# Routing spread over four steps with three sends in each, and the first norm's rows on ScalarE

## The chip, the cores and the metric

The kernel runs on one core of a Trainium2 chip. The metric is the device time of one execution in microseconds.

## The reference

64 sequences of 113 tokens with 128 features each. 36 tokens of a sequence come from a 96x96 image by a patch projection with shifted copies and a layer norm, 77 are text. Then an attention block and a block of experts, both on a layer norm and both with a residual:

```python
h = _L0_tok_ref(x, ...)                      # patches 16x16, shifted projections, layer norm
h = jnp.concatenate([h, txt], axis=1)        # (64, 36 + 77, 128)
h = h + _L0_attn_ref(_layernorm(h), ...)     # 8 heads of 64; scores and softmax in bfloat16
h = h + _L0_ffn_ref(_layernorm(h), ...)      # a shared expert and 3 of 16 experts per token

# in _L0_ffn_ref
affinity = sigmoid(xf @ gate_w.T)
_, sel = top_k(affinity + expert_bias, 3)
gating = sel_aff / (sel_aff.sum(-1) + 1e-9)
out = shared_out + einsum('tk,tkd->td', gating, sel_out)
```

## The kernel before

Each engine has its own program, written out by hand; semaphores tie them together. An engine works strictly in its program's order, so a wait holds up all that stands behind it on that engine.

**Stages.** First the image patches of eight octets (an octet is 8 sequences) are projected, normed and put into `h`. Then comes a loop of steps n = -8 to 66 (n = 8 o + k; `o` is the octet, `k` the place in it). A step works on many sequences at once, each at another stage. On step n, VectorE makes the normed row `xn` of sequence n + 8 (line 1304: row minus `mean1`, times `rs1`, both per token), TensorE transposes it (line 786), ScalarE copies the transpose to `xt` (997) and VectorE makes its rest (1331). TensorE makes q (one chunk of four sequences, into bank 1), k (bank 2) and later v (792) from `xt`, ScalarE copies q (989) and k (993). Sequence n gets its row maximum (VectorE, 1309), ScalarE doubles it to pairs (984), VectorE subtracts it (1314), ScalarE takes the exponential (1012). Sequence n - 1 gets its product with v; sequence n - 2 gets its output projection (TensorE 778), is added into `h` (VectorE 1324), gets the statistics of the second norm (1326, 1337), whose variance and power GpSimd makes (573, 575), and VectorE writes the normed row into `pay` (1360), the last of its program in a step that depends on GpSimd. Sequence n - 3 is transposed (812) and multiplied with the gate weights (836). A further matmul makes the scores of sequence n + 1 (830), which ScalarE copies (1018).

**Routing.** For each group q of four sequences VectorE chooses the three experts of each token: `route`, parts 0 to 11. Part 2 is four MAX8 (1174), part 3 four FIND_INDEX8 (1178), part 4 a cast (1181), part 5 a comparison of 113x192 (1185), part 6 the count of the chosen (1191) and a product, parts 7 to 11 small sums up to the gates. TensorE counts the ranks of the tokens within each expert (`ranks`, six small matmuls) and VectorE turns them into row numbers (`place`, parts 0 to 3, five instructions). A step has six points (0 to 5) between VectorE's other work where `routing` puts such parts in. Parts 0 to 5 stand in step n = 4q + 7, parts 6 to 11 in 4q + 8, the placement in 4q + 9 (for group 14 in 4q + 8). GpSimd then sends each sequence with three indirect DMAs, one for each choice (`send_rows`, line 606), 12 a group. `SENDS` gives the sends of each step of an octet: 0, 3, 3, 3, 3, 4, 4, 4; steps 64 and 65 have 3 and 9. The point of a send within GpSimd's step is 0, 1 or 2; points 0 and 1 come right behind line 575. Group 15 is routed and sent among the expert tiles.

**First norm.** GpSimd makes `rs1` for an octet with one power of 113x8 (`first_pow`, line 517) in step k = 6, for the octet after the next.

**Tables and tiles.** During steps 54 to 62 `full_table` derives the rows of the first 47 expert tiles from the first 12 groups. SyncE loads tiles of 256 rows (line 419) as soon as the table is there, ScalarE starts loading expert weights in step 64. In 93 tiles TensorE computes each tile (874, 885, 894), VectorE scales it and GpSimd scatters the rows (line 625). At the end everything is merged and written out.

Of the kernel before, what the change touches and what calls it, by code (L numbers as in the profile page):

```python
# [22 lines left out]
B = 64  # L23
# [8 lines left out]
OCT = 8  # L32
# [32 lines left out]
FULL_READ = {EARLY_B + 7: (("table", 2),), EARLY_B + 10: (("table", 5),), EARLY_B + 12: (("tab_done", 2),)}  # L65
FULL_AT = {EARLY_B + 6 + i: part for i, part in enumerate(((0,), (1, 2), (3, 4), (), (5, 6), (7, 8), (9, 10), (), (11,)))}
# [3 lines left out]
SENDS = (0, 3, 3, 3, 3, 4, 4, 4)  # L70
SENDS_LAST = (3, 9)
# [6 lines left out]
def build(nc, x, txt, w_feat, tok_bias, tok_gb, wq, wkv, wo, bo, gate_w, e_bias, w_ffn, out):  # L78
    ctx = ExitStack()
    with ctx:  # L80
# [74 lines left out]
        mean1 = sb("mean1", [128, B])  # L155
# [91 lines left out]
        for name in (  # L247
# [3 lines left out]
            "st1_raw st1_done mean1_done ve1_done rs1_done xn_ready xt_done xt_copied qa_done qb_done q_copied k_copied "  # L251
# [50 lines left out]
        def ok(n, end=B):  # L302

            return not isinstance(n, int) or 0 <= n < end

        def placing(o, k):

            lag = 8 if o == NOCT else 9
            return o * 2 + (k - lag) // GRP if (k - lag) % GRP == 0 and ok(o * OCT + k - lag) else None
# [132 lines left out]
        def _(pool):  # L442
# [71 lines left out]
            def first_pow(o):  # L514
# [3 lines left out]
                                        ALU.pow).then_inc(S["rs1_done"], 1)  # L518

# [70 lines left out]
            def send(o, k, point):  # L590

                if o < 1 or (o == NOCT and k >= len(SENDS_LAST)):
                    return
                sends, first = (SENDS_LAST, 0) if o == NOCT else (SENDS, 1)
                begin = sum(sends[:k])
                cuts = [0, 0, 0, sends[k]] if k % GRP == first or o == NOCT else [0, min(1, sends[k]), min(2, sends[k]), sends[k]]
                for at in range(begin + cuts[point], begin + cuts[point + 1]):
                    b, c = divmod(at, TOPK)
                    send_rows((o - 1) * OCT + b, c)
# [40 lines left out]
        def _(pe):  # L640
# [93 lines left out]
            def step(o, k):  # L734
# [28 lines left out]
                if n in FULL_AT and n <= EARLY_B + 12:  # L763
# [149 lines left out]
        def _(act):  # L913
# [49 lines left out]
            def step(o, k):  # L963
# [17 lines left out]
                if ok(n):  # L981
# [3 lines left out]
                                         ACT.Copy).then_inc(S["mx2_done"], 1)  # L985
                if ok(n + 4):
# [87 lines left out]
        def _(dve):  # L1074
# [7 lines left out]
            def first_stats(o, i):  # L1082
# [12 lines left out]
                nc.vector.tensor_copy(mean1[0:T, bass.ds(o * OCT, OCT)], mv1[0:T, :, 0]).then_inc(S["mean1_done"], 1)  # L1095
# [136 lines left out]
            def routing(o, k, point):  # L1232

                n, kk = o * OCT + k, k % GRP
                if kk == 3 and ok(n - 7) and n < B:
                    route(o * 2 + (k - 7) // GRP, ((k - 7) // GRP) % 2, point)
# [278 lines left out]
```

## Time and profile before

| | us |
|---|---|
| median of 3 runs | 939.87 |
| lowest, highest | 935.1, 944.38 |
| the profiled execution | 940.34 |
| its span | 938.6 |
| granted TensorE clock, mean | 0.86 |
| busy: TensorE | 693.4 (74%) |
| busy: VectorE | 592.6 (63%) |
| busy: ScalarE | 438.0 (47%) |
| busy: GpSimd | 547.7 (58%) |

The step of a sequence can be read from VectorE's row maximum, line 1309: it occurs once a step for n = 0 to 63. The first is at 76.02 us. A busy share over the whole span mixes the steps with the tiles; the share in one window says more. In a row the bracket at the end is the idle time of the engine just before, and who ended it. The end of a matmul is modelled, so the moment at which another engine goes on is the surer sign that it is done.

### The profile page before, as it was taken

To read this page: it belongs to the slowest core of one execution; us is meant where nothing else is said; L and a number is where in the kernel's file an instruction comes from. 1 tells how busy PE (TensorE), PEld (TensorE's weight loads), DVE (VectorE), ACT (ScalarE), POOL (GpSimd) and SP (SyncE) were. 2 spreads that over 40 slices of the span, in tenths; PEclk is the share of its full clock that TensorE was granted. 3 is DMA by queue.
4 is the path that set the end of the run, shared out by engine and by line. 5 is a ranking of instruction groups with operands and counts; after the bars stand their busy time and mean duration, and the time that the engine had idled before them with its cause. 6 is when DMAs were issued, how large, how long until landed. Compare 5 with 4: busy or idle time off the path is not lost.

```text
span 938.6 us, 19989 instructions
## 1 busy us (share of the span) xinstructions
PE 693.4 (74%) x6122; PEld 570.1 (61%) x6122; DVE 592.6 (63%) x2030; ACT 438.0 (47%) x1044; POOL 547.7 (58%) x696
## 2 busy tenths in 40 slices
PE   6657999898988989989897771787687786776100
PEld 5446887787777777777786560565555564666100
DVE  1697898898898878888888360443434443443254
ACT  2556787687776767767685320221222221221000
POOL 4452227866667676756756656555556555555464
PEclk9879999999999999989999585787778788797755
DMA  9710001100000010000104242445444444565297
GB/s 299 209 26 11 2 2 34 32 26 28 27 32 28 26 34 27 29 23 32 34 26 108 78 121 76 122 147 167 133 132 141 140 139 136 155 189 149 74 326 232
DMA packets 66444, 88.02 MB, mean 94 GB/s; under 512 B 11612, under 2 KB 58848, under 8 KB 66186
## 3 DMA queue, kind: packets, MB, share of 16 engines
q1 hardware_dynamic: 30420, 34.76, 13.5%
q10 hardware_dynamic: 23824, 28.68, 10.7%
q0 software_dynamic: 12096, 23.30, 7.4%
q8 instruction: 51, 0.84, 0.4%
q14 instruction: 53, 0.43, 0.2%
HBM read 57.32 MB, written 30.87 MB: 94 GB/s over the span
## 4 chain that ended last, share of the span: by engine, by line
PE 41%; DVE 17%; issue 12%; another core or an unknown queue 6%; POOL 5%; DMA 4%; ACT 2%; ACTq 1%; SPq 0%; DVEq 0%; POOLq 0%
PE bank L885 10%; PE bank L683 4%; PE bank L894 4%; PE bank L778 4%; DMA x2t<-expert_rows 3%; PE bank L830 3%; PE bank L723 3%; PE bank L750 2%; PE bank L874 2%; DVE mx L1309 2%; PE bank L724 2%; POOL dispatched L606 2%; DVE s L1314 1%; PE bank L792 1%
## 5 line engine op out<-in xcount | busy, mean ns | idle before, releaser
L625 POOL DMA_INDIRECT expert_rows<-yb,dst_i x186 | 182.2, 980 | 142.9 <-DVE yb L1446 91.4
L606 POOL DMA_INDIRECT dispatched<-pay,sloti x192 | 205.8, 1072 | 55.9 <-issue 54.1
L1436 DVE TENSOR_TENSOR hide<-bank,sge 128x256 f32<-128x256 f32 x93 | 39.4, 423 | 190.5 <-ACT sge L1051 138.2
L1046 ACT ACTIVATE xe<-bank 128x256 f32<-128x256 f32 x93 | 35.7, 384 | 213.3 <-remote 103.3
L885 PE MATMUL bank<-xe,kt 128*128 128x256 f32 (+1 forms) x296 | 80.0, 407 | 44.9 <-issue 44.7
L683 PE MATMUL bank<-xt,wqkv 128*128 128x452 f32 x384 | 103.7, 402 | 1.6 <-DVE xt L1331 1.2
L885 PEld LDWEIGHTS bank<-xe,kt 128*128 128x128 f32 x296 | 55.0, 226 | 52.9 <-issue 48.6
L683 PEld LDWEIGHTS bank<-xt,wqkv 128*128 128x128 f32 x384 | 70.6, 201 | 7.3 <-DVE xt L1331 1.4
L1309 DVE TENSOR_REDUCE mx<-s 113x8 bf16<-113x904 bf16 x64 | 69.6, 1088 | 6.4 <-ACT s L1018 5.6
L830 PE MATMUL bank<-kt,qt 64*113 64x113 f32 x1024 | 68.9, 272 | 4.6 <-DVE h L1324 3.6
L573 POOL TENSOR_SCALAR ve<-mv 113x1 f32<-113x1 f32 x64 | 14.8, 231 | 98.2 <-DVE mv L1337 96.9
L778 PEld LDWEIGHTS bank<-wo_r,ot 128*113 128x113 f32 x512 | 63.5, 187 | 6.8 <-ACT ot L973 2.9
L792 PE MATMUL bank<-wqkv,xt 128*113 128x512 f32 x192 | 60.7, 425 | 8.8 <-ACT qt L989 7.9
L830 PEld LDWEIGHTS bank<-kt,qt 64*113 64x113 f32 x1024 | 58.1, 176 | 12.9 <-issue 7.5
L1018 ACT ACTIVATE s<-bank 113x452 bf16<-113x452 f32 x128 | 63.2, 549 | 4.0 <-PE bank L830 3.9
L778 PE MATMUL bank<-wo_r,ot 128*113 128x128 f32 x512 | 62.4, 267 | 3.3 <-ACT ot L973 2.6
L978 ACT ACTIVATE pt<-bank 113x912 bf16<-113x912 bf16 x64 | 60.9, 952 | 3.9 <-PE bank L750 3.7
L1012 ACT ACTIVATE p<-s 113x904 bf16<-113x904 bf16 x64 | 60.7, 948 | 0.0
L1051 ACT ACTIVATE sge<-bank 128x256 f32<-128x256 f32 x93 | 35.6, 382 | 52.4 <-PE bank L885 33.8
L894 PE MATMUL bank<-kt,hide 128*128 128x128 f32 x252 | 45.8, 311 | 17.2 <-DVE hide L1436 14.5
L804 PEld LDWEIGHTS bank<-vf,pt 113*128 113x128 bf16 x512 | 47.2, 98 | 18.1 <-issue 18.1
L894 PEld LDWEIGHTS bank<-kt,hide 128*128 128x128 f32 x252 | 42.9, 221 | 25.1 <-DVE hide L1436 18.9
(209 smaller groups left out, 1829.3 us busy)
## 6 DMA issues: line engine op xcount, KB each, us to landing
kt<-in_w_ffn ACTq DMA_DIRECT2D x74, 192.0 KB
xs_all<-dispatched SPq DMA_DIRECT2D x77, 140.0 KB
x2t<-expert_rows SPq DMA_DIRECT2D x16, 672.0 KB
vr<-in_w_ffn ACTq DMA_DIRECT2D x35, 192.0 KB
out_h<-h ACTq DMA_DIRECT2D x16, 224.0 KB
x2t<-in_x ACTq DMA_DIRECT2D x4, 864.0 KB, 9.2
x2t<-in_x SPq DMA_DIRECT2D x4, 864.0 KB, 11.0
dispatched<-pay,sloti POOLq DMA_INDIRECT x192
```

The lines of the kernel that those rows point to most:

```text
L606: pool.indirect_dma_start(out=xs_dram[:, :], out_offset=bass.IndirectOffsetOnAxis(ap=sloti[:, q % (PAYS // GRP), b, c:c + 1], axis=0), in_ ...
L625: pool.indirect_dma_start(out=y_dram[:, :], out_offset=bass.IndirectOffsetOnAxis(ap=dst_i[:, slot, j:j + 1], axis=0), in_=yb[t % RW][:, j, ...
L683: m = nc.tensor.matmul(dst, wqkv[:, a, at:at + 128], xg[:, b, :], start=(j == 0), stop=(j == 2))
L778: m = nc.tensor.matmul(bank[3][0:T, 0:D], ot[k % 2][:, c, :], wo_r[:, a, c * D:(c + 1) * D], start=(c == a == 0), stop=(c == NC - 1 and a ...
L792: m = nc.tensor.matmul(bank[1][0:T, :], xt[gv][:, b, kv * T:(kv + 1) * T], wqkv[:, a, 2 * H * DH:], start=(j == 0), stop=(j == 2))
L830: m = nc.tensor.matmul(bank[3 + e][0:T, c * T:(c + 1) * T], qt[gs][half_p, c, ks * T:(ks + 1) * T], kt[gs][half_p, c, ks * T:(ks + 1) * T] ...
L885: m = nc.tensor.matmul(bank[3 - i][:, j * TR + i2 * cols:j * TR + (i2 + 1) * cols], w_ex[slot][i2][:, j * F:(j + 1) * F], xe[1 - i][:, i2 ...
L894: m = nc.tensor.matmul(bank[4 + i][:, j * D:(j + 1) * D], hide[i][:, j * 128:(j + 1) * 128], w_ex[(t - 2) % RW][j if loads(t - 2) == 2 els ...
L978: nc.scalar.activation(pt[(k - 1) % 2][0:T, :, 0:TP], bank[5][0:T, :].bitcast(BF16).rearrange("p (h t) -> p h t", h=H)[:, :, 0:TP], ACT.Co ...
L1012: nc.scalar.activation(p16[k % 2][0:T, :, :], s16[k % 2][0:T, :, 0:T], ACT.Exp).then_inc(S["exp_done"], 1)
L1018: m = nc.scalar.activation(s16[(k + 1) % 2][0:T, i:H:2, 0:T], bank[3 + i][0:T, 0:4 * T].rearrange("p (c t) -> p c t", t=T), ACT.Copy)
L1309: nc.vector.reduce_max(mx[i][0:T, :], s16[i][0:T, :, 0:T], AX.X).then_inc(S["max_done"], 1)
```

## The change

- Routing of a group takes three steps and its placement a fourth: parts 0 to 3 in step 4q + 7 (part 3 now between the attention output and the rest of v), 4 to 6 in 4q + 8, 7 to 11 in 4q + 9, `place` in 4q + 10. Group 13 is routed and placed by 4q + 9, group 14 by 4q + 8.
- `SENDS` is now a running total over the steps: three sends in every step from 11 to 58, four from 59 to 64, twelve in step 65.
- The early table's parts come one step later at first and two at the end of the list: 55 to 63.
- VectorE's line 1304 goes. ScalarE makes `xn` as Identity(rs1 * h + shift1), behind the pair maximum and ahead of the copy of q. VectorE writes the negated mean into `mean1`, and GpSimd multiplies it with `rs1` into `shift1`, once per octet, right behind `first_pow`.

Unchanged lines are left out of the diff below.

```diff
@@ -62,13 +62,19 @@
-FULL_READ = {EARLY_B + 7: (("table", 2),), EARLY_B + 10: (("table", 5),), EARLY_B + 12: (("tab_done", 2),)}
-FULL_AT = {EARLY_B + 6 + i: part for i, part in enumerate(((0,), (1, 2), (3, 4), (), (5, 6), (7, 8), (9, 10), (), (11,)))}
+FULL_READ = {EARLY_B + 8: (("table", 2),), EARLY_B + 11: (("table", 5),), EARLY_B + 14: (("tab_done", 2),)}
+FULL_AT = {EARLY_B + 7 + i: part for i, part in enumerate(((0,), (1, 2), (3, 4), (), (5, 6), (7, 8), (), (9, 10), (11,)))}
-SENDS = (0, 3, 3, 3, 3, 4, 4, 4)
-SENDS_LAST = (3, 9)
+PLACED = {4 * q + 10: q for q in range(NGRP - 3)}
+PLACED.update({B - 3: NGRP - 3, B: NGRP - 2})
+ROUTE = {7: ((0,), (1,), (2,), (), (3,), ()), 8: ((4,), (5,), (6,), (), (), ()), 9: ((7,), (8,), (9,), (), (10,), (11,))}
+PLACE = ((0,), (1,), (2,), (), (3,), ())
+ROUTE_SOON = {7: ROUTE[7], 8: ((4,), (5,), (6,), (), (7,), (8,)), 9: ((), (), (), (), (9, 10), (11,))}
+ROUTE_LAST = {7: ((0,), (1,), (2,), (3,), (4,), (5,)), 8: ((6,), (7,), (8,), (9,), (10,), (11,))}
+PLACE_LAST = ((), (0,), (), (1,), (2,), (3,))
+SENDS = [3 * max(0, min(n - 10, 48)) + 4 * max(0, min(n - 58, 6)) for n in range(B + 1)] + [B * TOPK - 12]
...
@@ -305,8 +311,7 @@
         def placing(o, k):
-            lag = 8 if o == NOCT else 9
-            return o * 2 + (k - lag) // GRP if (k - lag) % GRP == 0 and ok(o * OCT + k - lag) else None
+            return PLACED.get(o * OCT + k)
         def wait_y(eng, g, i):
...
@@ -516,6 +521,10 @@
+                after(pool, "mean1_done", o)
+                after(pool, "rs1_done", o)
+                nc.gpsimd.tensor_tensor(shift1[0:T, o * OCT:(o + 1) * OCT], mean1[0:T, o * OCT:(o + 1) * OCT],
+                                        rs1[0:T, o * OCT:(o + 1) * OCT], ALU.mult).then_inc(S["shift1_done"], 1)
             def patch_scale(o, i):
...
@@ -589,14 +598,13 @@
             def send(o, k, point):
-                if o < 1 or (o == NOCT and k >= len(SENDS_LAST)):
+                n = o * OCT + k
+                if not 0 < n < len(SENDS):
-                sends, first = (SENDS_LAST, 0) if o == NOCT else (SENDS, 1)
-                begin = sum(sends[:k])
-                cuts = [0, 0, 0, sends[k]] if k % GRP == first or o == NOCT else [0, min(1, sends[k]), min(2, sends[k]), sends[k]]
-                for at in range(begin + cuts[point], begin + cuts[point + 1]):
-                    b, c = divmod(at, TOPK)
-                    send_rows((o - 1) * OCT + b, c)
+                begin, end = SENDS[n - 1], SENDS[n]
+                cuts = [begin, min(begin + 1, end), min(begin + 2, end), end]
+                for at in range(cuts[point], cuts[point + 1]):
+                    send_rows(at // TOPK, at % TOPK)
             def send_rows(m, c):
...
@@ -760,7 +768,7 @@
-                if n in FULL_AT and n <= EARLY_B + 12:
+                if n in FULL_AT and n <= EARLY_B + 14:
...
@@ -983,6 +991,13 @@
+                if ok(n + 8):
+
+                    if k == 0:
+                        after(act, "shift1_done", o + 1)
+                    after(act, "xt_done", n + 8, -1)
+                    nc.scalar.activation(xn[k % 2][0:T, :], h[0:T, n + 8, :], ACT.Identity, bias=shift1[0:T, n + 8:n + 9],
+                                         scale=rs1[0:T, n + 8:n + 9]).then_inc(S["xn_ready"], 1)
                 if ok(n + 4):
...
@@ -1092,7 +1107,7 @@
-                nc.vector.tensor_copy(mean1[0:T, bass.ds(o * OCT, OCT)], mv1[0:T, :, 0]).then_inc(S["mean1_done"], 1)
+                nc.vector.tensor_scalar(mean1[0:T, bass.ds(o * OCT, OCT)], mv1[0:T, :, 0], -1.0, None, ALU.mult).then_inc(S["mean1_done"], 1)
             def token_stats(o):
...
@@ -1231,16 +1246,17 @@
             def routing(o, k, point):
-                n, kk = o * OCT + k, k % GRP
-                if kk == 3 and ok(n - 7) and n < B:
-                    route(o * 2 + (k - 7) // GRP, ((k - 7) // GRP) % 2, point)
-                if kk == 0 and ok(n - 8):
-                    route(o * 2 + (k - 8) // GRP, ((k - 8) // GRP) % 2, 6 + point)
+                n = o * OCT + k
+                for since in (7, 8, 9):
+                    q = (n - since) // GRP
+                    if (n - since) % GRP == 0 and 0 <= q < NGRP - 1:
+                        plan = ROUTE_LAST if q == NGRP - 2 else ROUTE_SOON if q == NGRP - 3 else ROUTE
+                        for part in plan.get(since, ((),) * 6)[point]:
+                            route(q, q % 2, part)
-                if q is not None and kk == 1 and point < 4:
-                    place(q, ((k - 9) // GRP) % 2, point)
-                if q is not None and kk == 0 and point in (1, 3, 4, 5):
-                    place(q, ((k - 8) // GRP) % 2, (1, 3, 4, 5).index(point))
+                if q is not None:
+                    for part in (PLACE_LAST if q == NGRP - 2 else PLACE)[point]:
+                        place(q, q % 2, part)
             def grp(a, g):
...
@@ -1294,15 +1310,6 @@
             def step(o, k):
-                if ok(n + 8):
-
-                    if k == 0:
-
-                        after(dve, "mean1_done", o + 1)
-                        after(dve, "rs1_done", o + 1)
-                    after(dve, "xt_done", n + 8, -1)
-                    nc.vector.tensor_scalar(xn[i][0:T, :], row(n + 8), mean1[0:T, bass.ds(n + 8, 1)], rs1[0:T, bass.ds(n + 8, 1)],
-                                            ALU.subtract, ALU.mult).then_inc(S["xn_ready"], 1)
                 if ok(n):
```

## Rows read from the trace of the kernel before

**Rows 1.** Windows, steps 32 to 39: stretch, length, busy PE PEld DVE ACT POOL, clock, DMA share, GB/s.

```profile
294.94:301.90 6.96, 6.96 (x75) 6.09 (x75) 6.40 (x20) 5.17 (x13) 5.59 (x8) 0.83 0.11 30
301.90:307.96 6.06, 6.06 (x81) 5.31 (x80) 5.85 (x18) 5.22 (x13) 1.77 (x3) 1.00 0.01 3
307.96:314.68 6.72, 5.88 (x75) 5.11 (x74) 4.98 (x13) 4.99 (x13) 4.82 (x7) 1.00 0.08 28
314.68:322.52 7.84, 6.65 (x76) 5.55 (x75) 7.18 (x29) 6.13 (x15) 5.22 (x7) 1.00 0.11 37
322.52:328.77 6.25, 6.00 (x74) 5.08 (x73) 6.08 (x21) 4.54 (x12) 4.20 (x7) 1.00 0.06 20
328.77:335.76 6.99, 6.25 (x80) 5.37 (x80) 6.10 (x20) 5.20 (x13) 4.20 (x6) 1.00 0.10 30
335.76:343.71 7.95, 7.09 (x79) 6.13 (x78) 5.26 (x13) 5.85 (x14) 6.76 (x9) 1.00 0.13 34
343.71:351.49 7.78, 5.58 (x71) 4.60 (x71) 6.59 (x30) 4.55 (x12) 6.26 (x9) 1.00 0.12 39
```

**Rows 2.** Timeline, VectorE: row maximum of steps n = 8 and n = 56.

```profile
127.87 1.09 DVE L1309 TENSOR_REDUCE mx<-s 113x8 bf16<-113x904 bf16 x1
...
465.64 1.08 DVE L1309 TENSOR_REDUCE mx<-s 113x8 bf16<-113x904 bf16 x1
```

**Rows 3.** Timeline, GpSimd, ends of steps 34 and 37 to step 38.

```profile
312.44 0.22 POOL L573 TENSOR_SCALAR ve<-mv 113x1 f32<-113x1 f32 x1 [0.92 <-DVE mv L1337]
...
337.43 1.40 POOL L606 DMA_INDIRECT dispatched<-pay,sloti  x1 [0.30 <-issue]
339.13 0.98 POOL L606 DMA_INDIRECT dispatched<-pay,sloti  x1 [0.30 <-issue]
340.11 1.71 POOL L517 TENSOR_TENSOR rs<-ve,half 113x8 f32<-113x8 f32 x1
...
342.20 0.24 POOL L573 TENSOR_SCALAR ve<-mv 113x1 f32<-113x1 f32 x1
```

**Rows 4.** Timeline, VectorE, ends of steps 38 and 39.

```profile
343.13 0.41 DVE L1360 TENSOR_SCALAR pay<-h,mv,rs 113x128 f32<-113x128 f32 x1 [0.81 <-POOL rs L575]
...
349.18 0.21 DVE L1345 RECIPROCAL rec<-bank 113x8 f32<-113x8 f32 x1 [0.93 <-remote]
...
350.71 0.35 DVE L1185 TENSOR_TENSOR wz<-iota,pay 113x192 f32<-113x192 f32 x1
350.98 0.34 DVE L1360 TENSOR_SCALAR pay<-h,mv,rs 113x128 f32<-113x128 f32 x1
351.24 0.34 DVE L1304 TENSOR_SCALAR xn<-h,mean,rs 113x128 f32<-113x128 f32 x1
351.49 1.09 DVE L1309 TENSOR_REDUCE mx<-s 113x8 bf16<-113x904 bf16 x1
```

**Rows 5.** Timeline, ScalarE, step 34.

```profile
309.08 0.22 ACT L984 ACTIVATE mx<-mx 113x16 bf16<-113x16 bf16 x1
309.21 0.53 ACT L989 ACTIVATE qt<-bank 128x452 f32<-128x452 f32 x1
...
311.36 0.27 ACT L997 ACTIVATE xt<-bank 128x113 fp32r<-128x113 f32 x1 [1.18 <-PE bank L786]
```

**Rows 6.** Groups of instructions, whole run: ScalarE with and without a scale operand.

```profile
L997 ACT ACTIVATE xt<-bank 128x113 fp32r<-128x113 f32 x64 | 17.2, 268 | 25.7 <-PE bank L786 22.1 <-issue 1.9 <-remote 1.6
L946 ACT ACTIVATE xs_all<-xs_all,trs 72x128 f32<-72x128 f32 x32 | 10.3, 391 | 14.2 <-POOL trs L526 14.2
```

**Rows 7.** Timeline, GpSimd and TensorE, start of the expert tiles.

```profile
530.58 1.15 POOL L606 DMA_INDIRECT dispatched<-pay,sloti  x1 [0.19 <-issue]
...
540.96 0.97 POOL L606 DMA_INDIRECT dispatched<-pay,sloti  x1 [0.30 <-issue]
...
543.29 1.04 POOL L625 DMA_INDIRECT expert_rows<-yb,dst_i  x1 [1.03 <-issue]
...
544.64 1.62 PE L885 MATMUL bank<-xe,kt 128*128 128x256 f32 x3 [3.73 <-issue]
```

## What the change does to the time, before it was run

> **What bounds the kernel now.** I read the time in three stretches: the start to the first row maximum, the 64 attention steps, and the expert tiles with their merge. The change touches the steps and the hand-over to the tiles, so I first cut one octet of steps into windows, each from one row maximum (line 1309) to the next [rows 1]. The reader is to see that the eight steps are unlike each other: 6.06 us for the shortest, 7.84, 7.95 and 7.78 us for steps 35, 38 and 39. The octet takes 56.55 us. Over the six octets from step 8 to step 56 the mean is (465.64 - 127.87) / 6 = 56.30 us [rows 2], so this octet stands for the others.
>
> No engine is full in all steps. TensorE is busy for all of step 33 but for only 5.58 of 7.78 us in step 39; VectorE is busy for 7.18 of 7.84 us in step 35, which holds six parts of the routing [rows 1]. Against step 34, which holds no routing (4.98 us of VectorE), the first six parts cost 1.61 us (step 39) to 2.20 us (step 35), the last six 1.10 us (step 36), and a placement 0.87 to 1.12 us (steps 33 and 37) [rows 1].
>
> The timeline of GpSimd shows the bound of step 38. It runs four sends, then the power of the octet ahead (line 517, 1.71 us), and only then the variance of the step (line 573) at 342.20 [rows 3], which is 6.44 us into the step. In step 34, with three sends and no power, the same instruction runs at 312.44, 4.48 us in, and waits for VectorE [rows 3]. VectorE's row for `pay` (line 1360) therefore idles 0.81 us for line 575 [rows 4]. So step 38 is bound by GpSimd.
>
> The third thing is TensorE's reports. In step 34 ScalarE waits 1.18 us for the transpose of line 786 until 311.36, 3.4 us into the step [rows 5]; in step 39 VectorE waits 0.93 us for a report of unknown source before line 1345 [rows 4]. Step 33, which has no send at its start (three GpSimd instructions in all), is the shortest [rows 1]. Sends and late reports go together in these rows; what joins them, they don't show.
>
> **Routing spread.** Each group of four loses nothing, it only moves: parts 4 and 5 leave the full step (35, 39) for the next, parts 7 to 11 leave that one for the third, the placement goes from the third to the fourth, which had none. In steps 35 and 39 part 5 takes 350.98 - 350.71 = 0.27 us of VectorE's order [rows 4]; part 4, a smaller tile, lies between 0 and that, and I take 0.10. The steps that take them in had VectorE waiting or TensorE busy. The placement in steps 34 and 38 adds 1.0 us to a VectorE that was busy 4.98 of 6.72 us [rows 1]; the cover is its own wait, and without it the step grows by up to that 1.0. TensorE's six rank products move along.
>
> **The row of the first norm.** VectorE loses line 1304: 351.49 - 351.24 = 0.25 us in each of 56 steps [rows 4]. ScalarE gains an activation of 113x128 with two operands from memory, which this trace does not hold. The nearest rows are 0.27 us for a copy of 128x113 with none and 0.39 us for 72x128 with one [rows 6]; another operand adds no more than the first did (0.12 us), so 0.27 to 0.51 us, and I take 0.39. ScalarE is busy 4.53 to 6.13 us of a step [rows 1], so it has room, but the place matters: behind the pair maximum (309.08) and ahead of the copy of q (309.21) [rows 5], and the products for v wait for that copy. Where VectorE or a late report bounds the step, this is hidden; in the two steps nearest to TensorE's bound I charge 0.1 each. GpSimd's multiply once per octet is near line 573, 0.22 to 0.24 us [rows 3]; with its wait, 0.35. The sign of the mean changes in one instruction per octet, at no cost. The first eight steps of filling now pass row, transpose and copy through ScalarE alone: 0 to 1 us, taken as 0.5.
>
> **Sends.** A send and its gap take (540.96 - 530.58) / 8 = 1.30 us [rows 7]. Steps 37 to 39 lose one each, and step 33 gets the three that step 32 now lacks. For step 38: 6.44 - 1.30 + 0.35 = 5.5 us into the step, or 5.8 if step 37 shrinks by 0.3; from there to the next maximum it is 343.71 - 342.20 = 1.51 us, less 0.25 [rows 3, 4], so 6.8 to 7.1. I take 6.95.
>
> Step by step, before [rows 1] and expected: 6.96 to 6.6; 6.06 to 6.2; 6.72 to 6.8; 7.84 to 7.2 (0.10, 0.27 and 0.25 off); 6.25 to 6.3; 6.99 to 6.7 (placement out, five small parts in, 0.25 off); 7.95 to 6.95; 7.78 to 7.2. The sum is 53.95 us, 2.6 less. Six octets give -15.6.
>
> **What is paid back.** The sends of a group start a step or so later, so more are left at the end: 12 in step 65 instead of 9. They run back to back in front of the first scatter of expert rows; in the run before, the last send starts at 540.96, the first scatter at 543.29, and TensorE, idle for 3.73 us, goes on at 544.64 [rows 7]. Three more are +3.9, which nothing covers. The steps from 57 on carry up to one send more each: +1.0. The early table comes up to two steps later; it is needed only at step 64, so it costs nothing.
>
> 940.3 - 15.6 + 3.9 + 1.0 + 0.5 = 930.1, so 930 us. The sum stands on the profiled execution (940.34 us, span 938.6), 0.5 above the median of the three runs; they spread over 935.1 to 944.4. A difference of about 1% (930.5 to 949.3) is what a measurement of this kernel can tell from none.
>
> **A rule against it.** In step 37's burst one send takes 1.40 us and its neighbour 0.98 [rows 3]. By it, moving the placement and part 6 beside GpSimd's work costs, and taking line 1304 off VectorE helps; the one long send would agree with it, and the rows don't show what it waited for.
>
> **Rivals.** (a) Reports late everywhere. With two sends running at each step's start, every step is like step 34: 6.7 at least. Sum 6.7 x 4 + 6.8 + 6.95 + 7.2 x 2 = 54.95, gain 1.6 an octet, end at 936. For it: step 34 against 33. Against it: step 36 begins with a send and takes 6.25.
> (b) ScalarE in the ring, slower than before. The row stands between the pair maximum and q, and if maximum, q, v products, scores and their copy are the ring in every step, 0.39 x 56 = 21.8 us come on top: 952. It eats the gain from 10.3 / 56 = 0.18 us a step on. Against it: ScalarE waits over 1 us in step 34 behind these copies.
> (c) The late reports go with the bursts of four. Then steps fall to near TensorE's own work, 6.2 to 6.5, about 50.5 an octet: 6 x 5.8 = 35 off, 911.
> (d) The port. Four instructions an octet, moved beside GpSimd, each lengthen one of its by 1.40 - 0.98 = 0.42 us [rows 3]; if all show, 10 us over six octets: 940, no change.
> (e) The spread does nothing because steps 35 and 39 wait for reports and not for VectorE: 1.2 an octet less gained, 937, counted with (a).
>
> **Chances.** Forecast (926 to 934) 0.50; (a) with (e) 0.18; (b) 0.13; (c) 0.12; (d) 0.07. Of the forecast's 0.50, 0.32 lies below 930.5. Faster by over 1%: 0.32 + 0.12 = 0.44; within 1%: 0.18 + 0.18 + 0.07 = 0.43; slower: 0.13. The range reaches to (c) and (d) and leaves out most of (b) and a part of (c): 912 to 943.
>
> **What would show it.** In the windows of an octet no step above 7.3 us, step 38 near 7; VectorE's `pay` in step 38 waiting under 0.3 us for line 575; the three sends of each step without a wait for the slots; an ACTIVATE of 0.3 to 0.5 us on ScalarE; the wait of q's copy for nothing. Twelve sends after step 65 and the first scatter 15 us behind the first of them. I am wrong if steps like 33 and 36 grow beyond 6.5 (a, b), if the time from pair maximum to v products grows by more than 0.2 and the step with it (b), or if no octet takes more than 52 (c).

## The result and the profile after

The changed kernel takes 929.79 us (median of 13 runs, 921.78 to 937.14) beside 944.38 us for the kernel before (13 runs, 934.42 to 955.4): a ratio of 0.989, 95% interval 0.985 to 0.993. The profiled execution took 925.62 us, its span is 923.8 us; before they were 940.34 and 938.6 us. The forecast was 930.0 us. Repetitions, in the experiments below, gave ratios of 1.000, 0.990 and 0.975.

Line numbers moved: the row maximum is line 1316 now, TensorE's transpose of `xn` is 794, ScalarE's row is 999, the sends are 614, the variance 582, the row for `pay` 1367.

The windows of steps 32 to 39 of the kernel after, which answer to [rows 1]:

```profile
core 0: us, PE busy (x) PEld busy (x) DVE busy (x) ACT busy (x) POOL busy (x), PEclk, DMA share, GB/s
285.93:292.57 6.64, 6.36 (x74) 5.37 (x75) 6.16 (x17) 5.22 (x14) 5.43 (x7) 1.00 0.10 31
292.57:299.32 6.75, 6.20 (x75) 5.18 (x75) 5.82 (x16) 5.65 (x15) 4.46 (x6) 1.00 0.09 31
299.32:306.12 6.80, 6.61 (x80) 5.50 (x79) 6.08 (x16) 5.55 (x15) 4.40 (x6) 1.00 0.09 28
306.12:313.26 7.14, 6.23 (x74) 5.11 (x73) 5.87 (x25) 5.83 (x15) 4.82 (x7) 1.00 0.11 29
313.26:319.87 6.61, 6.38 (x74) 5.37 (x75) 6.17 (x16) 5.22 (x14) 5.41 (x7) 1.00 0.09 30
319.87:326.64 6.77, 6.20 (x75) 5.18 (x75) 5.96 (x16) 5.65 (x15) 4.48 (x6) 1.00 0.10 32
326.64:333.60 6.96, 6.68 (x81) 5.58 (x80) 5.84 (x17) 5.66 (x15) 5.97 (x8) 1.00 0.10 31
333.60:339.94 6.34, 5.94 (x74) 4.86 (x72) 6.10 (x26) 5.71 (x15) 4.81 (x7) 1.00 0.09 30
sum 54.01, PE 50.60 PEld 42.16 DVE 47.99 ACT 44.49 POOL 39.78; mean PE 6.33 PEld 5.27 DVE 6.00 ACT 5.56 POOL 4.97
```

The octet takes 54.01 us for 56.55 before, and 53.95 were expected. The long steps are gone (7.84, 7.95 and 7.78 became 7.14, 6.96 and 6.34). But the two steps that were short, 33 and 36, grew: 6.06 to 6.75 and 6.25 to 6.61. Against the forecast, five of the eight steps are within 0.1 us; steps 33 and 36 are 0.55 and 0.31 us longer than foretold and step 39 is 0.86 us shorter, so that part of the right sum is errors that cancel.

GpSimd's timeline around step 38, then VectorE's row for `pay` in it, which answer to [rows 3] and [rows 4]:

```profile
328.18 1.00 POOL L614 DMA_INDIRECT dispatched<-pay,sloti  x1 [0.30 <-issue]
329.19 1.69 POOL L522 TENSOR_TENSOR rs<-ve,half 113x8 f32<-113x8 f32 x1
331.03 0.21 POOL L526 TENSOR_TENSOR shift<-mean,rs 113x8 f32<-113x8 f32 x1
...
331.62 0.23 POOL L582 TENSOR_SCALAR ve<-mv 113x1 f32<-113x1 f32 x1
...
332.99 0.34 DVE L1367 TENSOR_SCALAR pay<-h,mv,rs 113x128 f32<-113x128 f32 x1
333.60 1.09 DVE L1316 TENSOR_REDUCE mx<-s 113x8 bf16<-113x904 bf16 x1 [0.27 <-ACT s L1033]
```

The power comes behind three sends instead of four, the variance is at 331.62 - 326.64 = 4.98 us into the step instead of 6.44, and `pay` no longer waits for GpSimd. What the end of the step waits for now is ScalarE's copy of the scores (line 1033, 0.27 us).

The hand-over, which answers to [rows 7] (first and last of the twelve sends, the first scatter, TensorE):

```profile
514.64 1.09 POOL L614 DMA_INDIRECT dispatched<-pay,sloti  x1 [0.31 <-issue]
...
528.80 0.97 POOL L614 DMA_INDIRECT dispatched<-pay,sloti  x1 [0.30 <-issue]
...
530.38 1.05 POOL L633 DMA_INDIRECT expert_rows<-yb,dst_i  x1 [0.27 <-issue]
...
530.15 1.19 PE L893 MATMUL bank<-xe,kt 128*128 128x256 f32 x2 [3.90 <-issue]
```

The first scatter comes 530.38 - 514.64 = 15.7 us behind the first of the twelve sends, as foretold.

**Where the 14.8 us of span come from.** By the row maxima of steps 0, 8, 56 and 63, the first tile's `xe`, the first scatter and the span's end (before: 76.0, 127.9, 465.6, 511.8, 533.3, 543.3, 938.6; after: 74.2, 128.1, 447.3, 494.0, 517.2, 530.4, 923.8), the stretches changed by -1.8 (to the first row maximum), +2.0 (first octet), -18.5 (steps 8 to 56), +0.5 (steps 56 to 63), +1.7 (from there to the first `xe`), +3.2 (to the first scatter) and -1.9 us (to the end).

### The profile page after: what moved, and what is told of

It is laid out like the page before. It is cut to its first block, busy times and chain, and to the rows that moved or that the text cites. A ratio compares the mean times of both kernels' runs of the same rounds, so it can differ in the third digit from the quotient of the medians.

```text
span 923.8 us, 20003 instructions
## 1 busy us (share of the span) xinstructions
PE 690.7 (75%) x6122; PEld 564.1 (61%) x6122; DVE 582.3 (63%) x1966; ACT 458.7 (50%) x1108; POOL 553.4 (60%) x704
## 4 chain that ended last, share of the span: by engine, by line
PE 48%; another core or an unknown queue 10%; issue 9%; ACT 9%; DVE 6%; DMA 3%; ACTq 2%; POOL 1%; SPq 0%; DVEq 0%; POOLq 0%
PE bank L893 7%; PE bank L691 5%; PE bank L838 5%; PE bank L800 5%; PE bank L786 4%; PE bank L758 4%; DMA x2t<-expert_rows 3%; PE bank L902 3%; PE bank L731 3%; ACT pt L986 2%; PE bank L732 2%; PE bank L882 2%; PE bank L844 1%; ACT s L1033 1%
## 5 line engine op out<-in xcount | busy, mean ns | idle before, releaser
L614 POOL DMA_INDIRECT dispatched<-pay,sloti x192 | 203.0, 1057 | 53.3 <-issue 52.7
L1061 ACT ACTIVATE xe<-bank 128x256 f32<-128x256 f32 x93 | 35.6, 383 | 219.7 <-remote 104.1
L893 PE MATMUL bank<-xe,kt 128*128 128x256 f32 (+1 forms) x296 | 76.9, 395 | 41.0 <-issue 40.7
L691 PE MATMUL bank<-xt,wqkv 128*128 128x452 f32 x384 | 100.7, 393 | 6.2 <-issue 4.9
L691 PEld LDWEIGHTS bank<-xt,wqkv 128*128 128x128 f32 x384 | 68.2, 194 | 12.7 <-issue 6.7
L893 PE MATMUL bank<-xe,vr 128*128 128x256 f32 (+1 forms) x140 | 37.7, 405 | 36.6 <-issue 36.6
```

The source lines that it names most:

```text
L614: pool.indirect_dma_start(out=xs_dram[:, :], out_offset=bass.IndirectOffsetOnAxis(ap=sloti[:, q % (PAYS // GRP), b, c:c + 1], axis=0), in_ ...
L691: m = nc.tensor.matmul(dst, wqkv[:, a, at:at + 128], xg[:, b, :], start=(j == 0), stop=(j == 2))
L893: m = nc.tensor.matmul(bank[3 - i][:, j * TR + i2 * cols:j * TR + (i2 + 1) * cols], w_ex[slot][i2][:, j * F:(j + 1) * F], xe[1 - i][:, i2 ...
```

## The experiments

The theory after the result: the even sends and the spread routing are worth more than the forecast said, and ScalarE's row eats a part of it, because it stands in the ring of waits from one row maximum to the next (rival b at work). Twelve kernels ran, in three groups of four. The kernel before, run beside each group, took 932.21, 938.28 and 836.78 us. It was not profiled there: its one profile (940.34 us) and the first profile of the kernel after belong to the runs of the result, where its median was 944.38 us. So a length of steps of one of the twelve, set against one of these two profiles, compares across groups, and is an estimate; the ratios, and lengths within a group, are not touched by that.

### The parts of the change, one at a time

**The whole change again.**

> The whole change, as reference for the three parts run beside it. Both theories: ratio to the kernel before 0.989 +- 0.004, steps 8 to 56 taking 319 us against 338.

Measured: 935.7 us, ratio 1.000 (0.996 to 1.005), where both theories had 0.989. Its profiled execution is among its longer ones: 937.66 us, where the twelve lie between 921.98 and 939.98.

**Only the even sends**, from the kernel before:

```diff
-SENDS = (0, 3, 3, 3, 3, 4, 4, 4)
-SENDS_LAST = (3, 9)
+SENDS = [3 * max(0, min(n - 10, 48)) + 4 * max(0, min(n - 58, 6)) for n in range(B + 1)] + [B * TOPK - 12]
...
+                begin, end = SENDS[n - 1], SENDS[n]
+                cuts = [begin, min(begin + 1, end), min(begin + 2, end), end]
+                for at in range(cuts[point], cuts[point + 1]):
+                    send_rows(at // TOPK, at % TOPK)
```

> The kernel before with nothing changed but the sends: three in every step from 11 on, four from 59, twelve in step 65. My theory: step 38's bound by GpSimd goes (about 1.0 us an octet), the step that follows the one without sends gets late reports of its own, and the tail costs 3.9 us; ratio 0.997 to 1.002, steps 8 to 56 shorter by 4 to 8 us. Rival (the bursts of four make all the late reports): those steps shrink by 20 us or more and the ratio is 0.985 or less.

Measured: 924.11 us, ratio 0.989 (0.984 to 0.995). The windows of steps 34, 35, 38 and 39, and of steps 8 to 56:

```profile
302.24:308.44 6.20, 5.87 (x75) 5.10 (x74) 5.07 (x14) 4.99 (x13) 4.85 (x6) 1.00 0.09 31
308.44:316.20 7.76, 6.64 (x76) 5.56 (x75) 7.15 (x29) 6.19 (x15) 5.09 (x7) 1.00 0.13 36
...
329.25:335.85 6.60, 6.60 (x79) 5.84 (x78) 5.09 (x13) 5.91 (x14) 5.76 (x7) 1.00 0.10 31
335.85:342.59 6.74, 5.65 (x72) 4.73 (x71) 6.49 (x30) 5.23 (x13) 5.72 (x7) 1.00 0.08 28
...
130.13:448.99 318.86, 295.55 (x3579) 252.22 (x3578) 288.96 (x914) 251.28 (x577) 222.14 (x293) 1.00 0.09 28
```

The ratio lies between the two expected values. Steps 8 to 56 take 318.9 us for 337.8 before: in the profiles, the even sends alone give 18.9 us, as much as the whole change (319.2). The kernel with the old sends that was profiled in this group, the next one, takes 337.7 us, so this isn't the group's doing alone. The medians are 8.1 us apart; the sends pay some 5 us back at the end of the steps, which leaves about 13 us, so 18.9 is rather too much. Part of it is the clock: in the profile of the kernel before, 11 us of steps 8 to 56 are at a granted clock of 0.50, up to 5.5 us lost by TensorE at half its speed (an estimate), and with the even sends none are. Step 38 fell by 1.35 and step 39, which has all its routing still, by 1.04 us. Step 35 (7.76) stayed, and is the routing's to shorten.

**Only ScalarE's row**, from the kernel before:

```diff
+                    nc.scalar.activation(xn[k % 2][0:T, :], h[0:T, n + 8, :], ACT.Identity, bias=shift1[0:T, n + 8:n + 9],
+                                         scale=rs1[0:T, n + 8:n + 9]).then_inc(S["xn_ready"], 1)
...
-                    nc.vector.tensor_scalar(xn[i][0:T, :], row(n + 8), mean1[0:T, bass.ds(n + 8, 1)], rs1[0:T, bass.ds(n + 8, 1)],
-                                            ALU.subtract, ALU.mult).then_inc(S["xn_ready"], 1)
```

> The kernel before with nothing changed but the first norm's row, made by ScalarE with GpSimd's shift. My theory: 0.25 us less in the steps that VectorE bounds (three or four of eight), 5 us in all: ratio 0.992 to 0.997. Rival b (the row stands in the ring of pair maximum, q and v): 10 us or more slower, ratio 1.010 or more.

Measured: 936.22 us, ratio 1.005 (1.001 to 1.008), between the theory's and the rival's; steps 8 to 56 take 337.7 us. Beside the old bursts, the row on ScalarE gains nothing and loses almost nothing. But TensorE, which waited for no row in the kernel before, now does (window 128 to 420 us; the numbers behind the bar are busy time and mean ns, then the idle time just before, with what ended it):

```profile
L790 PE MATMUL bank<-ident,xn 113*128 113x113 f32 x41 | 12.7, 309 | 11.2 <-ACT xn L995 9.4 <-issue 1.5
```

**The whole change, the row given back to VectorE** (the last diff reversed, on the kernel after):

> The kernel after with the row given back to VectorE: routing spread and even sends alone. My theory: every step whose end VectorE sets gets 0.25 us back, 5 to 12 us over 48 steps: ratio 0.994 to 1.000. Rival b: without the row in ScalarE's order the kernel is faster than the whole change, 0.985 or less.

Measured: 914.4 us, ratio 0.982 (0.977 to 0.987), as rival b had it; steps 8 to 56 take 312.6 us, in an execution that is the longest of its six (923.6 us). So the spread routing adds 318.9 - 312.6 = 6.3 us to what the sends gave, and the row on ScalarE costs 6.6 us against the first profile of the kernel after and 23.1 us against the one beside it. Neither size is firm: the second group's kernel with VectorE's row, the same up to step 64, takes 319.4 us over these steps, as long as the first profile of the kernel after.

Why more against the one beside it: ScalarE's timeline in step 34, of the first profile of the kernel after, of the repetition of this group, and of the kernel with the row on VectorE:

```profile
300.19 0.94 ACT L986 ACTIVATE pt<-bank 113x912 bf16<-113x912 bf16 x1 [0.39 <-PE bank L758]
...
301.12 0.48 ACT L999 ACTIVATE xn<-h,shift,rs 113x128 f32<-113x128 f32 x1
301.50 0.53 ACT L1004 ACTIVATE qt<-bank 128x452 f32<-128x452 f32 x1
```

```profile
303.84 0.93 ACT L986 ACTIVATE pt<-bank 113x912 bf16<-113x912 bf16 x1 [0.97 <-remote]
...
304.77 0.48 ACT L999 ACTIVATE xn<-h,shift,rs 113x128 f32<-113x128 f32 x1
...
305.31 0.32 PE L794 MATMUL bank<-ident,xn 113*128 113x113 f32 x1 [0.65 <-ACT xn L999]
```

```profile
301.02 0.93 ACT L982 ACTIVATE pt<-bank 113x912 bf16<-113x912 bf16 x1 [0.45 <-PE bank L754]
...
301.95 0.54 ACT L993 ACTIVATE qt<-bank 128x452 f32<-128x452 f32 x1
```

ScalarE copies the transposed probabilities (986) ahead of the row. That copy waits for TensorE's report, 0.39 us in the one execution and 0.97 in the other, and the row stands behind it in ScalarE's program; in the second execution TensorE then idles 0.65 us for the row. With the row on VectorE, the same late report holds up nothing that TensorE needs in this place. The groups of lines for these two operations, window 128 to 420 us, in the first profile of the kernel after, the repetition, and the kernel with VectorE's row:

```profile
L986 ACT ACTIVATE pt<-bank 113x912 bf16<-113x912 bf16 x44 | 41.5, 944 | 10.9 <-PE bank L758 9.9 <-remote 1.0
L794 PE MATMUL bank<-ident,xn 113*128 113x113 f32 x44 | 13.6, 310 | 5.1 <-ACT xn L999 2.3 <-issue 2.2
```

```profile
L986 ACT ACTIVATE pt<-bank 113x912 bf16<-113x912 bf16 x43 | 40.5, 941 | 24.7 <-remote 17.7 <-PE bank L758 7.0
L794 PE MATMUL bank<-ident,xn 113*128 113x113 f32 x42 | 13.2, 314 | 17.5 <-ACT xn L999 17.1
```

```profile
L982 ACT ACTIVATE pt<-bank 113x912 bf16<-113x912 bf16 x45 | 42.5, 946 | 4.9 <-PE bank L754 4.9
L790 PE MATMUL bank<-ident,xn 113*128 113x113 f32 x45 | 12.8, 283 | 0.0
```

TensorE's wait for the row is 2.3 us in the first, 17.1 in the second, none in the third, and it goes with the copy's wait (10.9, 24.7, 4.9 us). The repetition's steps 8 to 56 take 335.7 us; besides these waits the granted clock fell to 0.78 to 0.82 in four of its steps (8.76, 7.70, 9.35 and 9.39 us long, some 8 us more than its other steps would take). So this execution shows the chain of waits, and its size is not to be taken from it. The waits aren't an effect of the low clock: with only ScalarE's row in the kernel before, all of TensorE's waits for the row stand in steps at a granted clock of 1.00. The low clock follows them. In step 40 of the repetition TensorE stands idle for the row, and two microseconds after it goes on, its clock is granted at 0.50, the lower of its two levels (1.2 of 2.4 GHz), from 349.2 to 356.0 us:

```profile
347.28 0.32 PE L794 MATMUL bank<-ident,xn 113*128 113x113 f32 x1 [1.26 <-ACT xn L999]
...
350.00:351.00 1.00, 1.00 (x14) 1.00 (x14) 1.00 (x2) 0.91 (x2) 0.85 (x1) 0.50 0.00 0
```

Three profiles with the whole change's steps have such stretches between steps 8 and 56: this one, and two of the second group (the third time, and the one with the last sends spread). There are eight stretches, and each begins 0.7 to 2 us after a wait of TensorE for the row of 1.03 to 1.35 us has ended. Some waits as long have none behind them. In the first profile of the kernel after, in its fourth run and in the six profiles with even sends and the row on VectorE or one step ahead, the longest wait of TensorE in these steps is 0.99 us, and the clock stays at 1.00. The kernel before has three such stretches, behind waits of 1.14 to 2.25 us for other tiles. So a late row can cost more than its wait. What made the reports later in one execution than in another of the same program isn't shown by either trace.

### The row's place, and the last group's sends

**The whole change, third time.**

> The whole change once more, beside the next three on their chip. If the first pair (0.989 and 1.000) differed by whether ScalarE's row comes in time, the profile has TensorE waiting for xn for over 15 us in steps 10 to 55 where the time is near 1.000, and for under 5 us where it is near 0.989.

Measured: 930.65 us, ratio 0.990 (0.987 to 0.994). The profiled execution took 938.09 us, near the 938.28 of the kernel before. For such a ratio over 15 us of TensorE's waits for the row were expected; there are 8.1 us. Its steps 8 to 56 take 331.1 us, and four of them, at a granted clock of 0.78 to 0.83, take 36.3 us where four of its others take 26.8 on average. Three stretches of low clock lie in them, each behind a wait for the row of 1.13 to 1.33 us. So the sum of these waits doesn't tell the time of an execution; the few long ones weigh most.

**The row one step ahead**, behind the copy of k, so that it doesn't stand ahead of its own transpose:

```diff
                     nc.scalar.activation(kt[1 - g][:, kk, :], bank[2][:, 0:GT], ACT.Copy).then_inc(S["k_copied"], 1)
+                if ok(n + 9):
+                    norm_row(n + 9)
```

> The whole change, with ScalarE's row made one step ahead, between its copies of k and of xt, and no longer between the pair maximum and q. Theory (the place costs): TensorE never waits for the row, q's copy follows the maximum as before, steps 33, 36 and 37 go back to 6.0 to 6.4 us, ratio 0.980 or less. Rival (ScalarE's added 0.4 us of work costs, wherever it stands): ratio as the whole change on this chip, within 0.005.

Measured: 924.27 us, ratio 0.986 (0.982 to 0.990). TensorE waits for no row any more. It is 0.7% below the kernel after beside it, 924.27 to 930.65 us, but the intervals overlap, and by the ratio, 0.004 below, it is the rival's range. Steps 33, 36 and 37 take 6.75, 6.46 and 6.71 us in its profile, not the 6.0 to 6.4 expected, and steps 8 to 56 take 317.6 us: other late reports remain (ScalarE's copy of k waits 8.7 us for an unknown source, window 128 to 420 us, for 3.9 in the first profile of the kernel after). The times don't settle the place; the steps without sends, below, do.

**The last group's twelve sends one per tile** instead of in one burst at a tile:

```diff
-                if t == SEND_AT:
-                    for b in range(GRP):
-                        for c in range(TOPK):
-                            send_rows(B - GRP + b, c)
+                for at in range(1 * (t - SEND_AT), 1 * (t - SEND_AT) + 1):
+                    if 0 <= at < GRP * TOPK:
+                        send_rows(B - GRP + at // TOPK, at % TOPK)
```

> The whole change, with the twelve sends of the last group one in front of each tile's scatter from tile 6 on, and not all in front of tile 6's. Theory (a burst of sends holds up the scatters and so the loads of the tiles behind): TensorE's idle time of 14 to 20 us near tile 11 goes down by 8 to 14 us, ratio 0.008 to 0.014 lower than the whole change on this chip. Rival (the loads there are late for another reason, or the time is lost again later): the same within 0.004.

Measured: 928.74 us, ratio 0.987 (0.981 to 0.992), within 0.004 of the whole change beside it, as the rival had it.

**The same with the row on VectorE.**

> Routing spread and even sends, the row on VectorE, and the last group's sends one per tile. If both findings hold and add up, ratio 0.970 to 0.976; if the tail's gain is lost again later, 0.982 as without it.

Measured: 924.73 us, ratio 0.987 (0.983 to 0.992). The longest gap before a tile's `xe`, 20.40 us in the first profile of the kernel after and 18.95 in the one beside, is 13.40 us with these sends spread and 9.20 us here; the time stayed within the intervals of the others. So a shorter gap there gave no shorter time. This is not the better version that the first group had promised (0.982).

### What a row costs on either engine

**ScalarE makes each row twice**, the first into a tile that nobody reads (the kernel after, with this added):

```diff
+                    nc.scalar.activation(again[k % 2][0:T, :], h[0:T, n + 8, :], ACT.Identity, bias=shift1[0:T, n + 8:n + 9],
+                                         scale=rs1[0:T, n + 8:n + 9])
```

> The whole change, and ScalarE makes every first norm's row twice, the first time into a tile that nobody reads. Theory: the row stands in the ring pair's maximum, pair's maximum, row, q's copy, v's copy, and its first copy cost about 6.6 us over steps 8 to 56 (319.2 us in the whole change, 312.6 us with the row on VectorE); the second has no slack left to be absorbed and costs its full 0.3 to 0.4 us in each of some 56 steps: +10 to +20 us against the whole change beside it (a ratio of 1.011 to 1.022 to it), steps 32 to 39 longer than 54.0 us by 2 to 3 us, and the waits of TensorE for xn above 8.8 us. Rival, that the spread between 0.989 and 1.000 of the whole change is the clock's alone and ScalarE's row costs nothing: within 0.5% of the whole change beside it.

Measured: 835.19 us, ratio 0.998 (0.994 to 1.002); it is 1.025 of the whole change beside it (815.05 us, below), more than the theory had.

**VectorE makes each row twice**, the same in the kernel with VectorE's row:

> The whole change with the row back on VectorE, and VectorE makes it twice, the first time into a tile that nobody reads. If VectorE's row costs 0.25 us of a step that VectorE ends, as the prediction charged in the change's favour, this is 0.25 us x 56 steps, up to +14 us against the kernel with the row once on VectorE (ratio 1.015). Theory now: VectorE is idle before its maximum in each step and the row before it is covered, so it costs under 3 us (ratio under 1.004 to that kernel).

Measured: 824.93 us, ratio 0.988 (0.981 to 0.994); it is 1.012 of the kernel with the row once.

**VectorE's row once, again.**

> The whole change with the row back on VectorE, again, beside the whole change. Theory: 0.7 to 1.8% under it (0.982 to the kernel before, steps 8 to 56 in 313 us). Rival, that 0.982 against 1.000 on the other chip was the chip's and the minute's: within 0.5% of the whole change.

Measured: 815.29 us, ratio 0.973 (0.967 to 0.979). It is level with the whole change beside it, as the rival had it.

**The whole change, fourth time.**

> The whole change, beside the three others. It came out at 0.989, 1.000 and 0.990 of the kernel before. Theory: 0.988 to 1.000, and its steps 8 to 56 in 319 to 331 us, longer by what TensorE waits for xn (2.5 us at 319.2, 8.8 us at 331.1, 22 us at 335.7) and by steps in which the clock falls below 0.85. Rival of the waits: they are an effect of the falls of the clock alone, and then a profile without a fall has none over 3 us.

Measured: 815.05 us, ratio 0.975 (0.969 to 0.982), with 296.3 us for steps 8 to 56: both below what was expected.

Here every kernel ran 10 to 13% shorter than in the other groups, the kernel before too, though on the same chip as the first group. The traces show where: ScalarE's copy of the probabilities never waits, and no wait of ScalarE in the steps is for an unknown source. The windows of steps 8 to 56 of these four, in the order above:

```profile
129.71:444.18 314.47, 298.91 (x3577) 250.18 (x3577) 281.15 (x866) 279.35 (x673) 224.82 (x298) 1.00 0.09 29
```

```profile
133.83:435.22 301.39, 291.26 (x3576) 249.04 (x3574) 291.17 (x960) 248.50 (x576) 236.65 (x292) 1.00 0.10 30
```

```profile
128.86:420.80 291.94, 284.87 (x3577) 248.38 (x3575) 284.08 (x914) 246.81 (x577) 222.92 (x292) 1.00 0.10 31
```

```profile
127.91:424.23 296.32, 291.12 (x3577) 249.49 (x3577) 277.01 (x866) 261.20 (x625) 224.90 (x297) 1.00 0.10 30
```

- The second row on ScalarE adds (314.47 - 296.32) / 48 = 0.38 us to each step. ScalarE's row lasts 0.49 us but the next instruction starts 0.38 us after it (301.12 to 301.50 above): the whole start-to-start time goes into the step. Rival (b)'s mechanism holds for what comes on top of the first row.
- The second row on VectorE adds (301.39 - 291.94) / 48 = 0.20 us, and 1.2% to the median. I had expected under 0.4%, that it was covered. That expectation fell: the 0.25 us a step of the prediction was nearer.
- Moving the row from VectorE to ScalarE costs (296.32 - 291.94) / 48 = 0.09 us a step where no report is late. By the doubled rows it would be 0.38 - 0.20 = 0.18, so half of it is absorbed. The medians show nothing of these 4.4 us: the tiles and the merge were longer in the one profiled execution with VectorE's row (330.4 us from the first `xe` to the end, 324.1 in the other), with the clock at 0.902 for the whole span against 0.913. Whether that is an effect of the row or of the moment stays open.

So the row on ScalarE costs from nothing to 2.3% of the time (914.4 to 935.7 us in the first group, 924.73 to 928.74 in the second with the last sends spread in both, 815.29 to 815.05 in the third). In the profiles it is least where no report is late, and largest where the clock falls behind TensorE's longest waits for the row.

**Before the first send.** The new sends start in step 11. The windows of steps 8 to 10, in the first profile of the kernel after, with VectorE's row (first group) and with ScalarE's row one step ahead (second group):

```profile
128.06:146.45 18.39, 18.27 (x226) 15.78 (x227) 16.78 (x48) 16.21 (x40) 3.61 (x9) 1.00 0.01 1
```

```profile
132.41:150.25 17.84, 17.84 (x227) 15.59 (x226) 17.36 (x52) 15.22 (x37) 3.61 (x9) 1.00 0.01 2
```

```profile
122.42:140.14 17.72, 17.72 (x226) 15.51 (x227) 16.77 (x48) 16.20 (x40) 3.60 (x9) 1.00 0.01 2
```

Here the groups agree (18.41 us in the kernel after's fourth run, 17.87 with VectorE's row in the third group), and the row's place shows: between the pair maximum and q it costs (18.39 - 17.84) / 3 = 0.18 us a step, what the doubled rows gave; the same row one step ahead, with the same work on every engine, costs nothing against VectorE's, and TensorE is busy all the time.

The late reports come with the sends, and need more than the sends. Steps 12 to 39, in the same first profile and fourth run:

```profile
152.73:339.94 187.21, 176.06 (x2087) 147.74 (x2087) 164.63 (x506) 155.45 (x365) 140.54 (x183) 1.00 0.10 30
```

```profile
152.60:325.57 172.97, 169.86 (x2087) 145.69 (x2087) 161.62 (x505) 152.41 (x365) 141.67 (x183) 1.00 0.10 33
```

The two executions were level up to the first send; with the same sends they part by 14.2 us in 28 steps.

What else it takes, the traces of one core don't show.

## Why the prediction was right, and where it was wrong

**The long steps.** Right in size: step 38 expected at 6.95, measured 6.96, with the wait for GpSimd gone; step 35 expected 7.2, measured 7.14. In step 38 the way to it was another: I had the variance at 5.5 to 5.8 us and 1.26 us from there to the maximum, and measured are 4.98 and 333.60 - 331.62 = 1.98 us, with ScalarE's copy of the scores last. GpSimd no longer bounds this step, and that 6.95 came out is luck.

**The sends.** The term was too small. I gave them step 38 and a third of a microsecond in step 37. Alone they took 18.9 us off steps 8 to 56 in the profiles, about 13 by the medians. Step 39 lost its 0.93 us report [rows 4] and step 34 half a microsecond, at an unchanged routing. Rival (c) had this part right, that late reports go with the bursts; its size, 35 us, was too large, since late reports stayed in evenly sent steps (0.39 us in step 34 above, and a step 35 of 7.14 us). On the third occasion, with no late report, the whole change's steps 8 to 56 were at 296.32 / 6 = 49.4 us an octet, below (c)'s 50.5.

**The routing.** Expected at 0.37 us in steps 35 and 39 and a shift elsewhere; measured at 6.3 us over 48 steps in the first group, 0.13 a step, near the forecast, though it fell elsewhere: step 37 lost 0.84 us (6.81 to 5.97) when the placement left it, and step 39 gained 0.46. Against rival (e), that the spread does nothing, stands a median that is 9.7 us lower (924.11 to 914.4) in the same group; the second group's 319.4 us leaves the size open.

**ScalarE's row.** The step that failed. I let VectorE's 0.25 us off count in four steps of an octet and charged ScalarE 0.1 us in two: a gain of 0.8 us an octet. Measured is a loss: 4.4 / 6 = 0.7 us an octet with no late report, the one comparison of profiles within a group that no low clock disturbs, and 6.6 / 6 = 1.1 across the first groups. I took the row as hidden "where VectorE or a late report bounds the step". But the late report is not cover: ScalarE's copy ahead of the row is what waits for it, so the row comes behind the wait and adds to it, and behind some of TensorE's longest waits for it (1.03 to 1.35 us) the clock fell, which the forecast had nowhere. Without any late report it costs by its place in the ring, 0.18 us in each of steps 8 to 10. The sign of the mean cost nothing, as said; GpSimd's multiply (0.21 us) was charged 0.35 us of step 38, where GpSimd no longer is the bound. The activation lasts 0.49 us, near the upper bound of the 0.27 to 0.51 and not the 0.39 taken; the 0.38 us that it holds up the next one is what counted.

**Sum of the two.** Sends and routing gave 25.2 us over steps 8 to 56 (337.8 to 312.6) for about 10.8 in the forecast; the row took back 6.6 instead of giving 4.8. Together 18.5 for 15.6. The two parts are estimates across groups; their signs are shown within one. The sum was right by errors of opposite sign, that is, by luck, and the signature had warned: steps 33 and 36 grew beyond 6.5 us, which I had named as the mark of (a) or (b). (a), that every step with sends at its start takes 6.7 at least, is out, since with VectorE's row steps 33 and 36 are at 5.98 and 6.15 us beside such sends; (b) was at work. It isn't the whole of these two steps: in the second group step 33 takes 6.47 us with VectorE's row too, and 6.75 with the row one step ahead.

**The payment at the end.** Twelve sends and the first scatter 15.7 us behind the first: right, +3.2 us for +3.9. The filling of the ring cost 2.0 us in the first octet, and the stretch before it gave back 1.8; +0.5 was the forecast. The steps from 57 to the first tile cost 2.2 us more instead of 1.0.

**The port.** Sends last 1057 ns on average after the change and 1072 before: nothing of rival (d)'s 10 us shows. The contention itself was there (below).

**The whole.** Three of four comparisons gave 0.975 to 0.990 and one 1.000. The forecast of 930 met the first of them; about 1% faster held on two of four occasions, and a chance of 0.43 for no change was not too large.

## What to carry to other kernels

Ask of an instruction that you move to a less busy engine what stands ahead of it there and waits: it inherits that wait, and a wait that "covers" it is no cover if it lies before it in the same program. Double the suspected instruction on either engine to price it: in a ring the second one cost its start-to-start time (0.38 us here), and the busy share, which said that ScalarE was idle half of the time, told nothing of it. That prices one more instruction; the one that was there may have been partly absorbed. Look also for a stretch of the same run without the disturbance: three steps before the first send showed the row's price and its place more plainly than any median. Sends issued in even small portions were worth more than the one bound that they visibly removed, and a sum that comes out right still has to be read term by term.

## What the runs showed of the hardware

**Late reports, and long waits in the tiles, come and go with the occasion.** From line 1061, `xe` in the tiles, in the first profile of the kernel after (window 517 to 923 us) and in its fourth run (489 to 812 us):

```profile
L1061 ACT ACTIVATE xe<-bank 128x256 f32<-128x256 f32 x93 | 35.6, 383 | 219.7 <-remote 104.1 <-PE bank L882 64.5 <-issue 37.4
```

```profile
L1061 ACT ACTIVATE xe<-bank 128x256 f32<-128x256 f32 x93 | 35.6, 383 | 159.5 <-PE bank L882 145.5 <-PE bank L893 6.9 <-issue 6.4
```

104.1 us of waits for an unknown source went to none with the same program, while the waits for bank L882 rose from 64.5 to 145.5 us; together the idle time before this line went from 219.7 to 159.5 us, and the stretch from the first `xe` to the end from 406.6 to 324.1 us. A change must be compared within one group of runs only; between the first and the third group, on one chip, the kernel before differed by 10% and the kernel after by 13%. What sets the occasion isn't shown.

**VectorE holds up GpSimd.** In the kernel with VectorE's row twice, GpSimd's timeline and VectorE's at the same time:

```profile
284.97 0.97 POOL L611 DMA_INDIRECT dispatched<-pay,sloti  x1 [0.30 <-issue]
286.01 0.26 POOL L593 TENSOR_SCALAR pay<-dest 113x12 f32<-113x12 f32 x1
286.43 2.01 POOL L611 DMA_INDIRECT dispatched<-pay,sloti  x1 [0.15 <-issue]
...
286.27 0.69 DVE L1319 TENSOR_TENSOR v<-vr 113x512 bf16<-113x512 f32 x1
286.87 0.63 DVE L1322 TENSOR_TENSOR s<-s,mx 113x912 bf16<-113x912 bf16 x1
```

One send takes 0.97 us, the next, which meets two VectorE instructions, 2.01 us. In the kernel with one row it is the small instruction of GpSimd that meets them in its place, 1.29 us instead of 0.26:

```profile
275.60 1.29 POOL L592 TENSOR_SCALAR pay<-dest 113x12 f32<-113x12 f32 x1
```

The mean of a send was 1168 ns with the row twice and 1044 with it once. The Trainium skill, SBUF — State Buffer, section Who interferes with whom, says that a VectorE instruction with two SBUF inputs contends with a GpSimd instruction that reads SBUF; both VectorE instructions here (1319 and 1322) have two, and the trace agrees. It also means that the 0.20 us of VectorE's second row may hold some of this.
